# Graph attention over 4096 nodes: from units of 512 rows by 1024 columns to units of 1024 rows by 512 columns, with half of the preparation between the products

## The reference

```python
x: (4096, 128) f32; adj: (4096, 4096) int32, 0 or 1; W: (128, 128); a: (256, 1)
h = maximum(layernorm(x), 0)
Wh = h @ W
e = (Wh @ a1)[:, None] + (Wh @ a2)[None, :]      # a1, a2: the halves of a
e = where(e > 0, e, 0.2 * e)
e = where(adj > 0, e, -9e15)
out = x + elu(softmax(e, axis=1) @ Wh)
```

## Time and profile before

| what | value |
|---|---|
| median of 3 runs | 272.17 us (270.87, 272.17, 274.17) |
| profiled execution: its span | 270.6 us |
| its own time | not given apart from its span; the median is 1.6 us above the span |
| mean granted clock of TensorE | 0.957 |
| busy: PE, PEld | 231.0 us (85%), 213.2 us (79%) |
| busy: DVE, ACT, POOL | 219.3 us (81%), 151.7 us (56%), 148.7 us (55%) |
| DMA | 71.62 MB, mean 265 GB/s |
| first product, last product | 61.85 us, 264.5 us |

### The profile page before, as it was taken

How to read it: one execution, slowest core, us unless ns; L and a number is a source line. 1 busy time by engine, 2 the same in 40 slices (tenths; PEclk the granted TensorE clock), 3 DMA queues, 4 the chain that set the end, 5 groups by cost and what they waited for, 6 DMA issues and landing times.

```text
span 270.6 us, 7004 instructions
## 1 busy us (share of the span) xinstructions
PE 231.0 (85%) x2740; PEld 213.2 (79%) x2740; DVE 219.3 (81%) x430; ACT 151.7 (56%) x154; POOL 148.7 (55%) x89
## 2 busy tenths in 40 slices
PE   0067268349999999999999999999999999999991
PEld 0057257338999999999999999999999999999990
DVE  3597983572888898889889888988898889789885
ACT  0145336769994349537951994298349537951002
POOL 1469969423462993299049807950993299042002
PEclk9999875958999999999999999999999999999997
DMA  5999500079999956995899499949986995000101
GB/s 148 411 409 409 203 0 2 4 307 367 408 400 411 406 224 228 416 409 226 344 409 409 143 416 410 406 148 417 409 323 235 412 410 220 0 0 1 39 0 41
DMA packets 18921, 71.62 MB, mean 265 GB/s; under 512 B 736, under 2 KB 992, under 8 KB 18912
## 3 DMA queue, kind: packets, MB, share of 16 engines
q1 hardware_dynamic: 17760, 69.41, 65.5%
q10 hardware_dynamic: 1152, 2.10, 2.0%
HBM read 69.40 MB, written 2.10 MB: 264 GB/s over the span
## 4 chain that ended last, share of the span: by engine, by line
PE 79%; DVE 8%; POOL 3%; ACT 3%; DMA 3%; issue 3%; SPq 0%; POOLq 0%; ACTq 0%; DVEq 0%
PE acc L798 41%; PE acc L800 21%; PE mask_t L766 12%; DMA x_sb<-in_x_dram 3%; PE acc L730 2%; DVE val L539 2%; POOL rstd L298 2%; PE acc L741 2%; ACT mask L396 1%; DVE gq_hi L534 1%; PE acc L792 1%; POOL hn L305 1%; DVE gq_word L536 1%; ACT g_row L388 1%; DVE v L549 1%
## 5 line engine op out<-in xcount | busy, mean ns | idle before, releaser
L588 DVE SCALAR_TENSOR_TENSOR words<-g_row,gq_word,mask_t 128x512 f32<-128x512 uint8 (+1 forms) x256 | 172.6, 742 | 31.4 <-PE acc L800 27.8
L798 PE MATMUL acc<-val,words 128*128 128x258 f16 x1024 | 177.5, 274 | 0.0
L800 PE MATMUL acc<-val,words 128*128 128x129 f16 x1024 | 174.4, 219 | 0.0
L798 PEld LDWEIGHTS acc<-val,words 128*128 128x128 f16 x1024 | 99.7, 97 | 13.1
L314 POOL TENSOR_SCALAR mask<-raw 128x1024 uint8<-128x1024 int32 (+1 forms) x32 | 93.2, 2933 | 15.5 <-DMA raw<-in_adj_dram 15.5
L800 PEld LDWEIGHTS acc<-val,words 128*128 128x128 f16 x1024 | 100.0, 98 | 0.4
L396 ACT ACTIVATE mask<-raw,step_bias 128x3072 uint8<-128x3072 int32 (+1 forms) x32 | 87.2, 2795 | 0.1
L766 PE MATMUL mask_t<-ident_b,mask 128*128 128x128 bf16 x528 | 36.4, 224 | 6.5 <-ACT mask L396 6.5
L330 POOL TENSOR_TENSOR num<-acc_sb 128x516 f32<-128x516 f32 x7 | 7.7, 1104 | 59.8 <-ACT acc_sb L438 59.8
L766 PEld LDWEIGHTS mask_t<-ident_b,mask 128*128 128x128 bf16 x528 | 32.6, 115 | 7.5 <-issue 7.1
L396 ACT ACT_TABLE_LOAD x8 | 10.3, 1283 | 35.1 <-issue 34.8
(11 more groups left out here) (71 smaller groups left out, 139.6 us busy)
## 6 DMA issues: line engine op xcount, KB each, us to landing
raw<-in_adj_dram SPq DMA_DIRECT2D x32, 2048.0 KB, 12.3
x_sb<-in_x_dram SPq DMA_DIRECT2D x4, 512.0 KB, 8.0
out_dram<-x_sb ACTq DMA_DIRECT2D x8, 256.0 KB, 3.3
a_row<-in_L_gnn_a_dram SPq DMA_DIRECT2D x1, 128.0 KB, 6.7
w_sb<-in_L_gnn_W_dram SPq DMA_DIRECT2D x1, 64.0 KB, 3.2
```

The source lines that it names most:

```text
L588: nc.vector.scalar_tensor_tensor(words[:, q // HALF, q % HALF, :], g_row[:, bass.ds(c * CHUNK, CHUNK)], gq_word[:, 1, k:k + 1], maskt_byte ...
L798: nc.tensor.matmul(acc[:, t, 0:2 * V], high, val[:, tile].rearrange("p e v -> p (e v)"), start=False, stop=False, skip_group_check=True)
L800: last = nc.tensor.matmul(acc[:, t, 0:V], low, val[:, tile, 0], start=False, stop=False, skip_group_check=True)
```

## The change

What it does, part by part. A chunk is now 1024 rows (8 tiles of i, `CT`), so there are 4 chunks (`C`), and a unit is 1024 rows by 512 columns, so a chunk has 8 units (`U`). A unit's `adj` comes as two DMAs of 1 MB with runs of 2 KB. All bytes are made by ACT, two passes of 2048 elements per unit (the first one of all by DVE); POOL makes none. `words` are tiles of 1024 rows, in a ring of 4. The sum of a tile of i is 129 columns wide, three tiles to a PSUM bank, and the product of high by (high, low) of 258 columns becomes two products of 129, with the high words as weights of each; the seed matmuls are gone, and DVE adds the seed when it takes the sums out of PSUM (`take_sums`). The row is centred and negated instead of normalised, and the deviation is applied by ACT when it copies the projection out of PSUM (`keep_projected`). Groups 0 and 1 (of 1024 nodes) are projected ahead of the first product; groups 2 and 3, the transposes ahead of them and the spreads of groups 1 to 3 stand between the products of chunk 0, as do the ACT steps that belong to them. `aux` is the one PSUM bank that all of these use in turn.

The diff, cut to what is spoken of:

```diff
-GT = 8
-GROUP = GT * P
-CT = 4
+BT = 4
+BLOCK = BT * P
+CT = 2 * BT
 CHUNK = CT * P
...
-    adj_v = adj.rearrange("(r p k q) (g j) -> g r k p q j", p=P, k=2, q=CT, j=GROUP)
...
+    adj_v = adj.rearrange("(c b p q) (u j) -> c b u p q j", b=2, p=P, q=BT, j=BLOCK)
...
+                nc.gpsimd.tensor_tensor(v32[:, g % 2], wh_sb[:, group(g), 0:F],
+                                        dv[:, group(g)].unsqueeze(2).broadcast_to([P, CT, F]), ALU.mult).then_inc(v32_ready, 1)
+                pool.wait_ge(vh_ready, g + 2)
+                nc.gpsimd.tensor_tensor(val[:, group(g), 1, 0:F], v32[:, g % 2], val[:, group(g), 0, 0:F], ALU.subtract
+                                        ).then_inc(vl_ready, 1)
+
...
-            def to_bytes(c, slots=range(RING), tiles=(POOL_TILES,) * RING):
-                for s in slots:
-
-                    act.wait_ge(raw_in[s], (c + 1) * 16)
-                    act.wait_ge(turned, c * RING + s + 1)
-
-                    nc.scalar.activation(mask[:, s, tiles[s]:CT], raw[:, s, tiles[s]:CT], ACT.Sigmoid, scale=64.0,
-                                         bias=step_bias[:, 0:1]).then_inc(act_bytes, 1)
...
+            def rectify(b):
+                act.wait_ge(ht_ps, b + 1)
+                if b >= 4:
+
+                    act.wait_ge(wh_ps, 3 * (b // 2 - 2) + 3)
+                nc.scalar.activation(h_t[:, b % 4], turned_bank(b), ACT.Relu, scale=-1.0).then_inc(ht_ready, 1)
+
+            def keep_projected(g, k):
+                t0, t1 = BANKS[k]
+                act.wait_ge(wh_ps, 3 * g + k + 1)
+                act.wait_ge(rstd_ready, 2 * g + 1 + (t1 > BT))
+                for t in range(t0, t1):
+                    i = g * CT + t
+                    last = nc.scalar.activation(wh_sb[:, i], projected(bank_of_group(g, k), PT)[:, t - t0], ACT.Identity,
+                                                scale=rstd[:, i:i + 1])
+                last.then_inc(wh_ready, 1)
...
+            def to_bytes(c, u, k):
+                n = c * U + u
+                act.wait_ge(raw_in[u % RING][k], (2 * c + u // RING + 1) * 16)
+                if not (isinstance(c, int) and c == 0 and u < RING):
+
+                    act.wait_ge(turned, n - RING + 1)
+                nc.scalar.activation(mask[:, u % RING, k * BT:(k + 1) * BT], raw[:, u % RING, k * BT:(k + 1) * BT], ACT.Sigmoid,
+                                     scale=64.0, bias=step_bias[:, 0:1]).then_inc(act_bytes, 1)
...
+            to_bytes(0, 0, 1)
+            high_values(0, 0, BT)
+            rectify(2)
+            high_values(0, BT, CT)
+            rectify(3)
+            for k in range(3):
+                keep_projected(1, k)
+            to_bytes(0, 1, 0)
+            to_bytes(0, 1, 1)
+            exponentials(1)
+            rectify(4)
+            high_values(1, 0, CT)
+            to_bytes(0, 2, 0)
+            to_bytes(0, 2, 1)
+            rectify(5)
+            to_bytes(0, 3, 0)
+            keep_projected(2, 0)
+            keep_projected(2, 1)
+            to_bytes(0, 3, 1)
+            keep_projected(2, 2)
+            exponentials(2)
+            to_bytes(0, 4, 0)
+            rectify(6)
+            high_values(2, 0, CT)
+            to_bytes(0, 4, 1)
+            rectify(7)
+            to_bytes(0, 5, 0)
+            for k in range(3):
+                keep_projected(3, k)
+            exponentials(3)
+            to_bytes(0, 5, 1)
+            to_bytes(0, 6, 0)
+            high_values(3, 0, CT)
+            to_bytes(0, 6, 1)
+            for k in range(2):
+                row_copy(1, k)
+            to_bytes(0, 7, 0)
+            for k in range(2):
+                row_copy(2, k)
+            to_bytes(0, 7, 1)
+            for k in range(2):
+                row_copy(3, k)
+            act.wait_ge(vh_ready, 2 + G - 1)
+            for g in range(G):
+                square(g)
...
+            def take_sums(c):
+
+                dve.wait_ge(hp_ready, c + 1)
+                for k, (t0, t1) in enumerate(BANKS):
+                    wait_bank(dve, c, k)
+                    nc.vector.tensor_tensor(num[:, t0:t1], acc_bank(k), seed_row[:].unsqueeze(1).broadcast_to([P, t1 - t0, V]), ALU.add
+                                            ).then_inc(acc_free, 1)
+                dve.wait_ge(acc_free, 3 * c + 3)
                 nc.vector.reciprocal(rz[:], num[:, :, F]).then_inc(rz_ready, 1)
 
...
+            dve.wait_ge(mean_ps, 1)
+            dve.wait_ge(consts, 6)
+            nc.vector.tensor_scalar(seed_row[:, 0:F], aux[:, 0:F], SEED / N, None, ALU.mult).then_inc(mean_ready, 1)
...
+            def product(c, u, q):
+                n = c * U + u
+                first = (u, q) == (0, 0)
+                pe.wait_ge(words_ready, 4 * n + q + 1)
+                tile = u * BT + q
+                for t in range(CT):
+                    if first and t % PT == 0:
+
+                        if isinstance(c, int) and c == 0:
+                            pe.wait_ge(wh_ready, 6)
+                        else:
+                            pe.wait_ge(acc_free, 3 * (c - 1) + t // PT + 1)
+                    high = words_h[:, q, t * P:(t + 1) * P, HI]
+                    low = words_h[:, q, t * P:(t + 1) * P, LO]
+                    nc.tensor.matmul(acc_tile(t), high, val[:, tile, 0, 0:V], start=first and t % PT == 0, stop=False, skip_group_check=True)
+                    nc.tensor.matmul(acc_tile(t), high, val[:, tile, 1, 0:V], start=False, stop=False, skip_group_check=True)
+                    last = nc.tensor.matmul(acc_tile(t), low, val[:, tile, 0, 0:V], start=False, stop=False, skip_group_check=True)
+                    if (u, q) == (U - 1, BT - 1) and t in (2, 5):
+                        last.then_inc(acc_done, 1)
+                last.then_inc(words_free, 1)
...
+                for q in range(BT):
+                    product(0, u, q)
+                    if q == 1:
+                        if u == 0:
+
+                            pe.wait_ge(ht_ready, 4)
+                            pe.wait_ge(first_row, 2)
+                        turn(0, u + 1)
+                    if (u, q) == (0, 3):
+                        pe.wait_ge(first_row, 1)
+                        turn_x(4)
+                    if (u, q) == (1, 2):
+                        pe.wait_ge(ht_ready, 5)
+                        turn_x(5)
+                    if (u, q) in ((1, 3), (2, 0), (2, 2)):
+                        k = ((1, 3), (2, 0), (2, 2)).index((u, q))
+                        pe.wait_ge(wh_ready, 6 + k)
+                        pe.wait_ge(ht_ready, 6)
+                        project(2, k)
+                    if (u, q) == (2, 3):
+                        pe.wait_ge(wh_ready, 9)
+                        turn_x(6)
+                    if (u, q) == (3, 1):
+                        pe.wait_ge(ht_ready, 7)
+                        turn_x(7)
+                    if (u, q) in ((3, 2), (3, 3), (4, 0)):
+                        k = ((3, 2), (3, 3), (4, 0)).index((u, q))
+                        pe.wait_ge(wh_ready, 9 + k)
+                        pe.wait_ge(ht_ready, 8)
+                        project(3, k)
+                    if (u, q) in ((4, 2), (4, 3), (5, 0), (5, 1), (6, 2), (6, 3)):
+                        k = ((4, 2), (4, 3), (5, 0), (5, 1), (6, 2), (6, 3)).index((u, q))
+                        if k == 0:
+                            pe.wait_ge(wh_ready, 12)
+                        else:
+                            pe.wait_ge(grow_ready, k)
+                        spread_words(1 + k // 2, k % 2, aux)
...
+                    if (u, q) == (7, 3):
+                        pe.wait_ge(grow_ready, 6)
+                        pe.wait_ge(wh_sum, G + 2)
+                        nc.tensor.matmul(aux[:, 0:F], ones[:].broadcast_to([P, P]), v32[:, 0, 0], start=True, stop=True
+                                         ).then_inc(mean_ps, 1)
...
-                                nc.tensor.matmul(acc[:, t, 0:2 * V], seed_w[:], mean_hl[:].rearrange("p e v -> p (e v)"),
-                                                 start=True, stop=False, skip_group_check=True)
-                            for q in range(HALF):
-                                tile = s * GT + half * HALF + q
-                                high = words_h[:, half, q, t * P:(t + 1) * P, HI]
-                                low = words_h[:, half, q, t * P:(t + 1) * P, LO]
-                                nc.tensor.matmul(acc[:, t, 0:2 * V], high, val[:, tile].rearrange("p e v -> p (e v)"),
-                                                 start=False, stop=False, skip_group_check=True)
-                                last = nc.tensor.matmul(acc[:, t, 0:V], low, val[:, tile, 0],
-                                                        start=False, stop=False, skip_group_check=True)
```

807 lines of the change are left out of this document (410 added, 397 removed).

## The result

The changed kernel takes 299.1 us, median of 4 runs (294.99 to 299.58), against 271.52 us before in the same session (269.5 to 274.17, 4 runs): a ratio of 1.097, 95% interval 1.086 to 1.108. Medians are over all runs; the ratios rest on the runs within 1.5% of the fastest of the same kernel (the others fell in the chip's slower state), and differ from the quotient of the medians by up to 0.6%. The prediction was 292 us, 7% slower, with a range of 270 to 301. The profiled execution of the changed kernel has a span of 297.0 us, against 270.6.

The account below looks back on a forecast made before the run. PE bounds the kernel, without gaps in the loop. First product at 29.7, chunk 0 94.5 us to 124.2, next product 129.2, chunks 1 to 3 to 280.8, end 10.4: 291.2, 1.6 above for the median: 292 us; range 270 to 301.

Parts of the forecast that it names:

- PE's waits for ACT's bytes: Chunk 0: PE idle ahead of `turn` of units 2 to 5 and 8; 4.5, 2.3, 5.4, 5.1 and 7.1 us.
- the 4 us ahead of chunk 1: Ahead of chunk 1's first product: PE idle 4 us, since DVE makes no words of chunk 1 before the mean.
- the walk: Chunk 0 followed from each `turn` to the next: 94.5 us where PE alone needs 59, done at 124.2.
- The rival of full overlap: Chunk 0: both engines run on despite the fixed order, loss under 15 us, all 257 us; chance 0.12.
- each wait above is for a step that can't begin earlier: Chunk 0: argument against full overlap; with no latencies and no slow clock the walk still ends at 277.
- The start: Preparation ahead of chunk 0: first product at 29.7, 32 us earlier than in the kernel before.
- `keep_projected` at 0.37 us a copy: ACT's copies of the projection out of PSUM: 0.37 us each, between plain copy 0.26 and activation with pointer 0.49.
- Chunk 1 ... 51.2 ... Chunk 2: 50.6: After chunk 0: chunk 1 takes 51.2 us, to 180.4, chunk 2 50.6, to 231.0; units without gaps.
- The loop's term: Steady loop: a unit 6.33 us against 6.24, 24 units 152 us against 152.5; each instruction adds 2.8 ns.
- The end: Behind the last product: DVE's three banks +8.0 us, then 2.4 to the end of the span, 10.4 together.
- rivals of weight loads: Products: 97 ns loads no longer hide, a product 2.3 us, all about 405 us; chance 0.04.
- slow transfers: Transfers in 2 KB runs at 250 GB/s: a unit takes 8.4 us, all about 314 us; chance 0.03.

Follow-up runs that it names:

- the four edits: Changed kernel with PE's loop written out, squares behind ACT's loop, mean's row behind three words, half of chunk 0's bytes (units 1 to 7) on DVE: 273.42 us (1.010).
- the orders of three engines: Changed kernel with its loop, squares, mean and bytes edits, plus POOL's, DVE's and ACT's steps reordered in chunk 0: 261.58 us (0.962).
- the last step: ACT's bytes and high values put between single rectifies and copies, against the kernel with POOL and DVE already reordered (265.85 us): 261.58 us.

## Why the prediction was right, and where it was not

**The mechanism was right.** Two queues in fixed orders, each waiting for the other, make chunk 0 long: by the traces, half of the bytes off ACT made it 4.2 us shorter, another order on ACT alone 1.75, and, with the four edits in, the orders of three engines together 11.6. PE's waits for ACT's bytes were worked out at 4.5 + 2.3 + 5.4 + 5.1 + 7.1 = 24.4 us; the trace has 22.2 in six waits. All of what the prediction placed is there: `turn(2)` at 41.8 (forecast 45.2), `turn(3)` 53.4 (57.9), `turn(4)` 65.8 (72.0), `turn(5)` 83.8 (88.6), `turn(8)` 113.7 (118.9), the clock low behind each of the waits of 4 us and more, the 4 us ahead of chunk 1 (4.16). Moving the squares, moving the mean, or taking bytes off ACT each gave back what the walk charged for it, and the slow clock behind it.

**The rival of full overlap falls for this order, and only for this order.** It needed a loss in chunk 0 under 15 us; 92.5 less PE's 59 are 33.5. With half the bytes on DVE, the squares moved and the orders changed, chunk 0 takes 68.8 us, a loss of 10. With ACT's order alone changed, chunk 0 still took 90.6 us. What the prediction called "each wait above is for a step that can't begin earlier" is true of the queues as written, not of the work.

**The start and the walk of chunk 0 were 4.8 us too long** (chunk 0 done at 119.4 instead of 124.2). 2.8 of it is the first product, at 26.9 instead of 29.7. One step of it was priced wrong: `keep_projected` at 0.37 us a copy. Five copies in a row took 1.41 us:

```profile
25.36 1.41 ACT L417 ACTIVATE wh_sb<-acc,rstd 128x130 f32<-128x130 f32 x5 [0.41 <-PE acc L787]
```

One lasts 0.37 (the group's mean is 369 ns), but the next begins 0.26 after it: (1.41 - 0.37) / 4. The prediction had 0.37 from one to the next; its lower end, 0.26, was right, 1.8 us for the 16 copies ahead of the first product. The walk also adds up generously: its steps as written give 0.1 to 0.3 us less per stretch than its positions, 1.1 us over chunk 0.

**The step that failed is "Chunk 1 ... 51.2 ... Chunk 2: 50.6".** It has PE go on from chunk to chunk without a gap, as before. Chunk 1 took 51.9 us. From its end to the end of the last product it is 110.3 us where 100.4 were forecast: 5.5 idle at the branch, 1.0 idle again at 188, 1.9 of slow clock in the unit behind the gap (9.36 us from turn to turn, less 6.41 and that 1.04), and the other 1.5 mostly the loop's price per unit. The wait at 188 is gone too where the loop is written out. The profile of before held no sign of it, since its body is short; the instructions could have been counted (16 + 96 matmuls a unit and eight units in a body, where before there were 80 and four).

**The loop's term was mis-sized.** "Each instruction adds 2.8 ns" came from pairs; with three matmuls of 129 columns it is (172.5 - 161.3) / 3 = 3.7 ns. A unit is 6.41 instead of 6.33 us, 1.9 us over 24 units.

**The end was right:** 10.1 us behind the last product, forecast 10.4.

**That the number lay in the range was in part luck.** The sum of what differs from the forecast's span: -4.8 for the start and chunk 0, +0.3 for the gap ahead of chunk 1, +0.7 for chunk 1, +9.9 for the rest, -0.3 for the end: +5.8, from 291.2 to 297.0. Two misses of opposite sign stand in it, one of them, the branch, of a kind that the prediction did not have at all; with the start and chunk 0 as long as forecast, the time would have been 303.9, above the range. Without the branch, with PE's loop written out, 290.6 us were measured, close to the forecast of 292. The rivals of weight loads and of slow transfers are out: loads have 99 to 101 ns busy in the changed kernel and are hidden, and where the transfers had to catch up they ran at 385 GB/s.

## What to carry to other kernels

Work that is slid between the products of another engine pays only if each queue can run ahead of the one that it waits for: put the steps that release the bottleneck first, and let nothing that waits for the bottleneck stand ahead of them. To see what an order costs, walk the queues against each other, from one wait to the next, with durations from the profile; here it came within 3 us of the time for each order, though for the last step alone (8.8 forecast, 4.3 measured) it was wrong by half. The four edits (the loop written out, squares, mean, bytes) brought the change from 10% slower to 1% slower, the orders from there to 4% faster. When a loop's body grows, count its instructions.

## What the hardware showed that was not expected

A branch back cost PE 5.0 us with a body of 2592 matmuls and weight loads and 5.5 (5.47 to 5.56 in five traces) with one of 1792, and nothing with 1296 or 648, and it is followed by slow clock. It shows as idle time with the releaser "issue" and as packets on the queue of instructions. Splitting a matmul of 258 columns into two of 129 cost 6 ns each time, twice what the gaps between longer ones suggest.

A DVE operation of 8 or 16 columns took 2.1 to 2.4 us instead of 0.2 while POOL worked on 1024 columns of SBUF, in the changed kernel (at 91.44 and 93.73 us) and with the new orders. The 4.02 us before the change are of the same kind: that operation ended at 29.93, and an operation of POOL at 29.90:

```profile
24.52 5.38 POOL L314 TENSOR_SCALAR mask<-raw 128x2048 uint8<-128x2048 int32 x1
```

Two more follow it, of 16 and of 8 columns, 2.01 us (to 31.97) and 5.34 us (to 37.31), with POOL's next two ending at 31.94 and 37.27; behind that, with POOL idle from 37.27 to 39.94, the same operations take 0.2 each. That makes over 10 us of DVE's time in the preparation. It does not happen each time that the two overlap: the same five operations took 0.2 each from 42.86 to 43.64, while POOL worked on 1024 columns (L314, from 41.96, 2.77 us).

No run here takes POOL's work away, so the cause is only argued. The Trainium skill, SBUF — State Buffer, section SBUF: two separate sides, has DVE (with two SBUF inputs or in a two-port mode) and POOL take one pair of ports by a lock that is held for the whole instruction; the trace agrees where the operations are long: 72.03 + 2.37 = 74.40 is 0.04 us behind POOL's 71.96 + 2.40. The trace does not agree at 43.14, where DVE subtracts one tile of SBUF from another in 0.18 us beside that operation of POOL.
